# Windowed attention with router and experts: shift rows kept as fp32 words, and the block maxima transposed later on TensorE

## What is computed

```
x = x + attn(layernorm(x));  x = x + ffn(layernorm(x))

attn: q, k, v = projections of y, 16 heads of 16; window of 64 keys, causal
    scores = einsum("bhqd,bhkd->bhqk", q, k) * scale + bias   # bias 0 or -inf
    attn = softmax(scores, axis=-1);  out = attn @ v;  return out @ Wo.T
ffn: scores = sigmoid(x @ gate_w.T + lb_bias); the best 2 of 8 experts by token
    weight of an expert = mean of its tokens' normalised scores
    out = sum of the chosen experts' gated MLPs (inner width 128) * weight
    out = out + shared gated MLP (inner width 256)
```

## Time and profile before

| | |
|---|---|
| median of three runs | 533.08 us (532.95 to 533.52) |
| the profiled execution | span 533.3 us; its own time is not listed apart from the three |
| granted TensorE clock over the span | 0.986 |
| TensorE (PE), weight loads (PEld) | 502.2 us (94%), 420.7 us (79%) |
| VectorE (DVE), ScalarE (ACT), GpSimd (POOL) | 406.6 (76%), 335.8 (63%), 227.8 us (43%) |
| attention sweep | about 20 to 329 us, groups 4 to 13 alike |

### The profile page before, as it was taken

One profiled execution on the slowest core, in us unless ns is written; L12 is line 12 of the kernel. 1 busy time (PEld: TensorE's weight loads), 2 busy tenths in 40 slices (PEclk: granted clock), 3 DMA queues, 4 the chain that ended last, 5 costly groups with the idle time before them and its releaser, 6 DMA issues.

```text
span 533.3 us, 16306 instructions
## 1 busy us (share of the span) xinstructions
PE 502.2 (94%) x5561; PEld 420.7 (79%) x5561; DVE 406.6 (76%) x1268; ACT 335.8 (63%) x776; POOL 227.8 (43%) x418
## 2 busy tenths in 40 slices
PE   7799899999999999999999988989998999999997
PEld 4567678778777777777777765778898999999996
DVE  6566878988988988998997877784676777764764
ACT  3577767867877777767867743331687888772111
POOL 5100110332542542552452355870466666763650
PEclk8899999999999999999999999998999999999999
DMA  6071011032132133122212114486656565637993
GB/s 213 10 226 52 4 41 42 14 103 94 34 103 92 35 103 92 41 97 92 75 34 73 64 44 173 180 248 206 213 179 184 155 184 170 193 116 254 399 396 136
DMA packets 42559, 68.85 MB, mean 129 GB/s; under 512 B 9708, under 2 KB 28655, under 8 KB 42480
## 3 DMA queue, kind: packets, MB, share of 16 engines
q1 hardware_dynamic: 33984, 43.17, 25.7%
q0 software_dynamic: 6480, 17.31, 9.3%
q10 hardware_dynamic: 2016, 7.34, 4.0%
HBM read 36.40 MB, written 32.06 MB: 128 GB/s over the span
## 4 chain that ended last, share of the span: by engine, by line
PE 81%; DVE 12%; issue 3%; POOL 2%; ACT 1%; POOLq 0%; DVEq 0%; ACTq 0%
PE ps L556 40%; PE ps L615 8%; PE ps L645 5%; PE ps L811 5%; DVE rmax L1197 4%; PE ps L626 4%; PE ps L610 3%; PE ps L892 3%; PE ps L567 2%; PE ps L654 2%; PE ps L631 2%; PE ps L660 2%; DVE xs L1230 2%; PE ps L699 2%; PE ps L909 2%
## 5 line engine op out<-in xcount | busy, mean ns | idle before, releaser
L500 POOL DMA_INDIRECT z_slots<-z,slot x64 | 64.2, 1003 | 121.5 <-PE ps L615 101.2
L556 PE MATMUL ps<-wF,wA 128*128 x639 | 102.8, 303 | 0.9 <-DVE wA L1526 0.8
L1197 DVE TRANSPOSE_TENSOR_REDUCE rmax<-ps 128x32 f32<-128x1024 f32 x64 | 79.6, 1244 | 17.1 <-PE ps L615 16.7
L541 POOL DMA_INDIRECT y_rows<-vm,dest x71 | 69.6, 980 | 52.7 <-issue 29.0
L556 PEld LDWEIGHTS ps<-wF,wA 128*128 128x128 f32 x639 | 85.1, 189 | 3.0 <-issue 2.0
L991 ACT ACTIVATE probs<-ps 128x1024 f32<-128x1024 f32 x64 | 65.5, 1024 | 30.7 <-PE ps L631 28.7
L556 PE MATMUL ps<-yT,wA 128*128 128x256 f32 x384 | 69.7, 309 | 1.5 <-DVE yT L1170 1.5
L615 PE MATMUL ps<-bd,kT 64*128 64x256 f32 x512 | 66.6, 380 | 0.0
L556 PEld LDWEIGHTS ps<-yT,wA 128*128 128x128 f32 x384 | 54.4, 200 | 4.6 <-issue 1.9
L615 PEld LDWEIGHTS ps<-bd,kT 64*128 64x128 f32 x512 | 49.8, 191 | 5.2
L1095 ACT ACTIVATE vt<-ps 128x256 f32<-128x256 f32 x32 | 12.2, 383 | 56.9 <-PE ps L556 55.0
(11 more groups left out here) (197 smaller groups left out, 1140.0 us busy)
## 6 DMA issues: line engine op xcount, KB each, us to landing
z<-z_slots SPq DMA_DIRECT2D x71, 136.0 KB
zT_scratch<-zT SPq DMA_DIRECT2D x16, 512.0 KB
bd<-y_rows SPq DMA_DIRECT2D x8, 512.0 KB, 10.3
out<-xs SPq DMA_DIRECT2D x16, 256.0 KB, 7.3
wraw_of<-wffn SPq DMA_DIRECT2D x10, 384.0 KB, 3.7
xs<-x SPq DMA_DIRECT2D x7, 512.0 KB, 3.9
wA<-zT_scratch ACTq DMA_DIRECT2D x7, 512.0 KB, 5.4
shift<-negs SPq DMA_DIRECT2D x128, 2.0 KB
```

Of the source, the lines that this page charges most:

```text
L500: eng.indirect_dma_start(z_slots, bass.IndirectOffsetOnAxis(ap=slot[:, c, j, t:t + 1], axis=0), z[:, c, t, :], None, bounds_check=E * REGI ...
L541: eng.indirect_dma_start(y_rows, bass.IndirectOffsetOnAxis(ap=dest[:, m:m + 1], axis=0), yo[:, m, :], None, bounds_check=K * T - 1, oob_is ...
L556: mm = eng.matmul(out, lhsT(a), rhs(b), start=start and n == 0, stop=stop and n == 2, skip_group_check=skip)
L1197: eng.tensor_reduce(rmax[:, n % 2, 0:32], S[n % 2].rearrange("p a (c q) -> p (a c) q", q=32), AX.X, ALU.max, apply_transpose=True).then_in ...
```

## The change

`shift` becomes fp32, and `shiftb` is a view of it as bf16 with a last index of 0 for the low and 1 for the high half of each word. `negs` goes, `neglo` (fp32, zeroed at the start by GpSimd) comes. The hi part is no longer computed: the first DMA copies `negm` itself as words of fp32, and `shift_of` reads the high halves, which are `negm` cut to bf16. The lo part is `negm` minus its own high halves, written as bf16 into the high halves of `neglo`. The semaphore `s_nh` goes, and the first DMA waits for `s_nm`. On TensorE the transpose of the block maxima stands behind all six products of the first chunk instead of behind three, and in step 3 behind the router's logits instead of ahead of them. The 12 matmuls at the start read the low halves.

```
-        shift = sb("shift", [P, 2, HPT * WIN], BF16)
+        shift = sb("shift", [P, 2, HPT * WIN])
+        shiftb = shift[:, :, :].bitcast(BF16).rearrange("p a (c two) -> p a c two", two=2)
-        negs = sb("negs", [2 * 32, 2, 32], BF16)
+        neglo = sb("neglo", [32, 2, 32])
+        negmb, neglob = (n[:, :, :].bitcast(BF16).rearrange("p a (c two) -> p a c two", two=2) for n in (negm, neglo))
...
-                    for part, ready in enumerate((s_nh, s_nl)):
+                    for part, (ready, rows) in enumerate(((s_nm, negm), (s_nl, neglo))):
                         eng.wait_ge(ready, b + 1)
                         eng.dma_start(shift[32 * part:P:64, pb, :].rearrange("m (a c) -> m a c", c=32),
-                                      negs[32 * part:32 * part + 32, pb, :]).then_inc(s_mr[pb], 16)
+                                      rows[:, pb, :]).then_inc(s_mr[pb], 16)
...
+                chain(eng.memset(neglo[:, :, :], 0.0))
                 eng.memset(shift[:, :, :], 0.0).then_inc(s_pad, 1)
...
-                        mm = eng.matmul(S[n % 2][:, c, :], onesb[64 * c:64 * c + 64, :], shift[64 * c:64 * c + 64, n % 2, :],
+                        mm = eng.matmul(S[n % 2][:, c, :], onesb[64 * c:64 * c + 64, :], shiftb[64 * c:64 * c + 64, n % 2, :, 1],
...
                         if project:
-                            project(g + 1, (0,), (0,))
+                            project(g + 1, (0,))
...
+                        if n == 3 and ahead and old >= 2:
+                            eng.wait_ge(s_x2, TPG * g)
+                            logits_by_experts(g - 2)
                         if ahead or n < BPG - 1:
                             if n == 0 and old == 3:
                                 eng.wait_ge(s_sl, g - 3)
                             maxima_T(b + 1, n2)
-                        if project:
-                            project(g + 1, (0,), (1,))
-                        if n == 3 and ahead and old >= 2:
-                            eng.wait_ge(s_x2, TPG * g)
-                            logits_by_experts(g - 2)
...
-                        eng.matmul(ps[:, 2, :], shift[:, 0, 0:P], shift[:, 1, :], start=True, stop=True)
+                        eng.matmul(ps[:, 2, :], shiftb[:, 0, 0:P, 0], shiftb[:, 1, :, 0], start=True, stop=True)
...
-                    eng.tensor_copy(negs[0:32, n % 2, :], negm[:, n % 2, :]).then_inc(s_nh, 1)
-                    eng.wait_ge(s_nh, b + 1)
-                    eng.tensor_tensor(negs[32:64, n % 2, :], negm[:, n % 2, :], negs[0:32, n % 2, :],
+                    eng.tensor_tensor(neglob[:, n % 2, :, 1], negm[:, n % 2, :], negmb[:, n % 2, :, 1],
                                       ALU.subtract).then_inc(s_nl, 1)
```

More of the change, by code:

```diff
@@ L214, in layer @@
         s_S, s_R, s_RT = sem("scores_in_psum"), sem("block_maxima"), sem("maxima_transposed")
-        s_nm, s_nh, s_nl = sem("neg_max"), sem("neg_max_hi"), sem("neg_max_lo")
+        s_nm, s_nl = sem("neg_max"), sem("neg_max_lo")
         s_mr = [sem("mrow_loaded_0"), sem("mrow_loaded_1")]
```

## The result

| | before | changed kernel |
|---|---|---|
| median | 533.02 us (4 runs, 532.20 to 533.52) | 520.06 us (4 runs, 519.56 to 521.69) |
| ratio | | 0.9743 (95% interval 0.9714 to 0.9772) |
| span of the profiled execution, granted clock | 533.3 us, 0.986 | 518.7 us, 0.997 |
| TensorE matmuls, weight loads | 502.2 us, 420.7 us | 492.7 us, 412.9 us |

The kernel became 13.0 us (2.6%) faster. The sign was right and the size was not.

A forecast was written before the change was run, and what follows sets the result against it. TensorE, busy 94% of the span, was taken as the bound, so only its few idle places counted. Terms 0.8 + 0.8 + 0.4 + 0.4 - 0.45 + 0.4 + 0 + 0.65 = 3.0 us gave 530.1 us, range 527.7 to 532.4.

The forecast's parts named there:

- TensorE gains the wait: Steps 0 to 2, transpose behind six products: TensorE saves only its visible wait, 0.09 us per steady group, about 0.8 in all.
- steps 1 and 2 of group 0, step 0 of group 1: Transpose comes 0.35 us later, the cast's 0.20 is saved, so 0.15 us is lost three times: -0.45.
- Step 0: Steady groups: z's normalisation holds VectorE, negated maximum starts 0.15 us later; without the cast the landing is 0.05 us earlier.
- Step 3: Logits ahead of the transpose fill the 0.34 us gap; DMA landing hands most back, gain about 0.08 us, ten groups 0.8.
- gap kept: Rival, step 3: earlier transfer misses the scatters' packets, takes 1.6 us, VectorE keeps up; 527.5 us, chance 0.13.
- Rows of 128 bytes: Shift-row DMAs with 128-byte instead of 64-byte rows, 32 descriptors as before: taken to cost nothing.
- The strided read: Shift product reads every second bf16, 128 matmuls, 0.22 us of path a pair: taken to cost nothing.
- The rival at half rate: Strided reading halves the shift product's rate, 0.44 us per pair in all 64 blocks: 544.1 us, chance 0.06.
- The late transpose: Rival: VectorE's chain sets the transpose of o in steady steps too, 39 x 0.15 = 5.9 us lost: 536.0, chance 0.03.
- The cast: VectorE's cast goes: lo part and both DMAs 0.20 us earlier, from transpose to landing, 64 times; worth depends on who waits.
- Prologue: Zeroing neglo costs 0.2 us, the first block's cast gains 0.2: sum 0; zeroing shift counted by elements, nothing more.
- First groups and tail: Step 0 of group 0: 0.4; three steps of groups 0 and 1: -0.45; their steps 3: 0.4; tail: 0.65.

## Why the prediction was wrong, step by step

**The step that failed** is "TensorE gains the wait: 0.07, 0.01, 0.01 us in a steady group". It came to 0.32, 0.21, 0.21, which is 9.3 us of the profile's difference where the sum had 0.8. The terms, beside the differences of the same stretches in the two profiles:

| term | forecast | profiles |
|---|---|---|
| steps 0 to 2, groups 2 to 14 (with steps 1 and 2 of group 1) | 0.8 | 9.3 |
| step 3, groups 4 to 13 | 0.8 | 0.2 |
| step 3, groups 2 and 3 | 0.4 | 0.4 |
| step 0 of group 0 | 0.4 | 1.2, of which some 0.8 is the half-clock stretch of before |
| steps 1 and 2 of group 0, step 0 of group 1 | -0.45 | 0.0 (forecast as a loss) |
| step 3 of groups 0 and 1 | 0.4 | 0.5 |
| prologue, to block 0's shift product | 0 | 1.5, the half-clock stretch around 10 us |
| tail (step 3 of group 14, group 15) | 0.65 | 0.6, and 0.9 behind block 63 |

One row makes the miss. The 0.07 and 0.01 were the chain's rows "issue" and the missing brackets of the matmul timeline. Both are measured from the modelled end of the matmul before, and matmuls overlap by more than half their length, so a wait of up to 0.16 us fits inside an end. The evidence against it stood in the same chain (0.33 us for this transpose, 0.11 for the others) and in the weight loads (49 waits against 17), and I read neither. I costed the products at their distance from one another, 0.12 us, and the transpose at nothing since it only moved; its price on the path, which held the wait, fell from 0.33 to 0.11. (The 0.8 is itself loose: 13 groups at 0.09 us make 1.2, and only with the smaller waits of 0.04 throughout 0.8.)

The Trainium skill, "Perfetto Trace Analysis", section "Identifying the Most-Contended Engine", says that the busy share of matmuls is no good measure of how near a kernel is to its limit, because pipelined instructions look smaller in the trace, and points to the busy share of the weight loads, beside another measure. This trace agrees: 98% by matmuls in the sweep before, 77% by weight loads (150.28 of 195 us).

**Step 0** was costed from one engine's side. I had the landing 0.05 us earlier there and left it out of the sum. The cast's 0.2 us, VectorE's z, the moved products and the logits of the step before act on it together: the products and logits alone gave nothing, the data alone 0.14 us, data and products 0.20, all three 0.32.

**Step 3** was right in that the gap is filled and the landing becomes the bound. Two sizes inside it were off, in opposite directions. The logits' 0.47 us were set against a gap of 0.34, so that the transpose would come 0.13 us later; it comes 1.52 us behind the step's shift product in both kernels (means of the nine groups), as the 0.34 too was counted from a modelled end. And the landing took 2.02 us from the issue instead of 1.82 (medians of steps 3), which takes back the 0.20 us of the cast. What is left is 0.03 us, not 0.08. The longer landing came with the data: the kernel with the data alone has 2.02 us, with both orders alone 1.82. There the second issue moved from 0.69 us after a scatter's issue to 0.48 after one, and 0.04 us is what the rows of 128 bytes cost in the other steps; which of the two makes the rest no run tells apart. The rival "gap kept", which had the earlier transfer miss the scatters, went the other way; its premise, that the scatters cost the transfer its extra time, was shown by the run with the scatters apart.

**Rows of 128 bytes** were taken at nothing. In steps 0 to 2 issue to landing went from 1.57 to 1.61 us in the median, 0.03 to 0.04. The estimate by the Trainium skill, "DMA: Bandwidth & Descriptors", section "Anatomy of one DMA — SWDGE (gpsimd) path", was 0.005; the measurement decides, and it did not matter in the sum.

**The strided read** costs nothing that matters. Shift matmuls have a mean of 389 ns against 380, and the pair still takes 0.22 us of path where it waits for nothing. The Trainium skill, "SBUF — State Buffer", section "Door 1: The DMA port swizzle", gives full bandwidth for at least two accesses to a line of 16 bytes; the trace agrees, with four. The rival at half rate would have shown 0.44 us per pair.

**The late transpose** did not reach TensorE: steps 1 and 2 kept at 4.77 us. The cover was there.

**The cast:** VectorE has 1204 instructions as forecast, and without it the lo part follows the negated maximum by 0.32 us (204.28 to 204.60 in step 3, where it was 0.51 in the earlier trace rows). The data change was worth 4.2 us by itself, half of it in step 0 (15 x 0.14 = 2.0), where the sum had nothing for it.

**Prologue:** the zeroing of `shift` as fp32 takes 956 ns against 951, so it goes by elements, as I took it. `neglo` costs 0.15 us and a link of 0.05. **First groups and tail** came out near their terms where the clock was the same, but for the loss of 0.45 us in three steps of groups 0 and 1, which came to nothing: there too the transpose comes only 0.17 to 0.28 us later behind the shift product and not 0.35, for the same hidden wait, and the cast's 0.20 covers that. What lies behind block 63, 0.9 us, isn't assigned: before has two half-clock stretches of 3.4 us there, and after one.

## What to carry to other kernels

On TensorE a wait shorter than a matmul's overlap (here 0.28 - 0.12 = 0.16 us) shows neither as an idle bracket nor as "issue". Before costing a moved instruction at its visible wait, compare starts with starts (here 0.28 us ahead of the transpose against 0.12 among the products), look whether its path price in the chain is its full length (0.33 against 0.11), and read the waits of the weight loads beside those of the matmuls. Where several chains hold a step, the parts of a change don't add up (0.14 and 0 alone, 0.32 together), and a gain can turn up in the step after the one in which it is made.

## What was not expected of the hardware

- A scatter of GpSimd issued 0.48 us ahead lengthened a 4 KB transfer issued by SyncE from 1.61 to 2.02 us (medians, step 3, with the scatter moved away and not).
- TensorE lost 0.04 to 0.05 us more than the wait itself, after waits of 0.16 and of 0.04 us alike.
- The start of this kernel comes in two lengths, block 0's shift product at about 19.8 to 20.2 or 21.3 us, by whether a stretch at the granted clock of 0.50 (1.2 GHz) falls around 10 us: the five profiles with one have 21.3, the eight without it the others; both lengths occur among kernels that hardly differ, and the 1.5 us between them is larger than some effects under study.
